# Graph layers with row gathers: one tile in 32 of the second layer is fetched row by row by SP and ACT instead of by POOL

## The reference, cut to what matters

```
h  = relu(layernorm(x))
m  = relu(concat(h[src], edge_attr) @ W_msg.T + b_msg)          # layer 0, per edge
m  = relu(m @ W_msg2.T + b_msg2)
x  = x + concat(h, segment_sum(m, dst) / count) @ W_apply.T + b_apply

h  = relu(layernorm(x))
a  = softmax of edge_weight over the edges of one dst           # layer 1, per edge
agg = segment_sum(a[:, None] * h[src], dst);  agg = agg / (|agg| + 1e-9)
c  = 0.5 * (h @ W_self + b_self + agg @ W_nb + b_nb);  c = c / (|c| + 1e-9)
x  = x + layernorm(c) * gamma + beta
```

## Time and profile before

| | |
|---|---|
| median of 3 runs | 11857.36 us |
| span of the profiled execution | 8618.0 us |
| the profiled execution's own time | not given beside its span |
| layer 1, gathers | 4389.7 to 8438.8 us |
| busy in the span: POOL, PE, DVE, ACT | 6262.0, 4989.1, 4066.7, 1112.8 us |

### The profile page before, as it was taken

The page is one execution under the profiler, slowest core; times in us unless marked ns, Lnnn a source line. Parts: engine busy times, 40 slices in busy tenths (PEclk is TensorE's granted clock), DMA queues, the critical chain, the costliest instruction groups (busy, mean ns, idle before and its releaser), DMA issues.

```text
span 8618.0 us, 124772 instructions
## 1 busy us (share of the span) xinstructions
PE 4989.1 (58%) x31459; PEld 4420.3 (51%) x31459; DVE 4066.7 (47%) x14617; ACT 1112.8 (13%) x1842; POOL 6262.0 (73%) x6528
## 2 busy tenths in 40 slices
PE   4777777777777777777744444444444444444444
PEld 3666666666666666666643333333333333333333
DVE  7555555555555555555553333333333333333336
ACT  2222222222222222222210000000000000000001
POOL 2777777777777777777657777777777777777772
PEclk9999999999999999999965555555555555555555
DMA  5332323233223333333332222222222222222222
GB/s 169 86 77 74 80 74 78 78 79 78 74 73 80 78 80 78 80 85 105 76 101 65 65 67 64 54 53 53 53 53 53 53 53 53 53 53 53 53 53 70
DMA packets 393788, 614.77 MB, mean 71 GB/s; under 512 B 171659, under 2 KB 249223, under 8 KB 392839
## 3 DMA queue, kind: packets, MB, share of 16 engines
q0 software_dynamic: 206848, 424.04, 19.2%
q1 hardware_dynamic: 186888, 190.15, 8.0%
HBM read 577.78 MB, written 35.92 MB: 71 GB/s over the span
## 4 chain that ended last, share of the span: by engine, by line
POOL 69%; issue 25%; PE 2%; DVE 2%; DMA 1%; DVEq 0%; SPq 0%; POOLq 0%; ACT 0%; ACTq 0%
POOL rows_ring L446 69%; PE bank L900 1%; PE bank L1028 0%; DVE acc L620 0%; DVE acc L609 0%; DMA rows_ring<-p_table,idx 0%; POOLq L191 0%; DVE stat L592 0%; SPq L338 0%; DVEq L609 0%; DVE acc L841 0%; DMA idx<-in_src_ring 0%; PE bank L891 0%; DVE work L874 0%; PE bank L897 0%
## 5 line engine op out<-in xcount | busy, mean ns | idle before, releaser
L446 POOL DMA_INDIRECT rows_ring<-p_table,idx x3232 | 3141.5, 972 | 1130.5 <-issue 1122.1
L446 POOL DMA_INDIRECT rows_ring<-h_table,idx x3232 | 3065.7, 949 | 1028.2 <-issue 984.3
L766 DVE TENSOR_TENSOR acc<-acc,bank 128x128 f32 x6464 | 1820.5, 282 | 2517.4 <-PE bank L900 2501.4
L900 PE MATMUL bank<-onehot,rows_ring 128*128 128x128 f32 x6464 | 1649.2, 435 | 2339.8 <-DMA rows_ring<-h_table,idx 2339.8
L900 PEld LDWEIGHTS bank<-onehot,rows_ring 128*128 128x128 f32 x6464 | 1417.4, 323 | 2571.6 <-issue 2242.3
L769 DVE TENSOR_SCALAR onehot<-iota,dloc,coef 128x128 f32<-128x128 f32 x6464 | 2286.3, 355 | 1.3 <-issue 1.2
L782 DVE TENSOR_TENSOR work<-bank,rows_ring 128x512 f32<-128x512 f32 x808 | 558.5, 691 | 1922.0 <-DMA rows_ring<-p_table,idx 1565.8
L900 PE MATMUL bank<-onehot,work 128*128 128x128 f32 x6464 | 935.1, 288 | 245.8 <-DVE onehot L769 239.2
L900 PEld LDWEIGHTS bank<-wmat,work 128*128 128x128 f32 x7264 | 983.4, 198 | 51.7 <-DVE acc L841 9.8
L900 PE MATMUL bank<-wmat,work 128*128 128x128 f32 x7264 | 987.7, 281 | 12.0 <-DVE acc L841 10.4
L900 PEld LDWEIGHTS bank<-onehot,work 128*128 128x128 f32 x6464 | 790.5, 193 | 387.4 <-DVE acc L766 348.3
(11 more groups left out here) (119 smaller groups left out, 782.9 us busy)
## 6 DMA issues: line engine op xcount, KB each, us to landing
work<-in_edge_t SPq DMA_DIRECT2D x404, 256.0 KB
rows_ring<-p_table,idx POOLq DMA_INDIRECT x3232
rows_ring<-h_table,idx POOLq DMA_INDIRECT x3232, 2.5
idx<-in_src_ring SPq DMA_DIRECT2D x404, 8.0 KB
ht_rows<-rows_ring SPq DMA_DIRECT2D x25, 256.0 KB, 2.1
p_table<-rows_ring SPq DMA_DIRECT2D x25, 256.0 KB, 2.2
work<-ht_rows SPq DMA_DIRECT2D x25, 256.0 KB, 2.6
h_table<-work SPq DMA_DIRECT2D x25, 256.0 KB, 2.3
```

What stands on the lines that cost most here:

```text
L446: pool.indirect_dma_start(out=rows_ring[:, 16 * h + G * k + j, :], out_offset=None, in_=table[:, :], in_offset=bass.IndirectOffsetOnAxis(a ...
L766: dve.tensor_tensor(win, win, ps_agg[k % 2][:, j * P:(j + 1) * P], ALU.add).then_inc(added, 1)
L900: ins = pe.matmul(tiles(dst)[t], left[t], right[t] if isinstance(right, list) else right, start=bias is None and n == 0, stop=n == len(pai ...
```

## The change

In layer 1 the last tile of every superblock (the fourth of its eighth group) isn't gathered by POOL. Its 128 source numbers lie in a new input `src_last`, one line of 128 per superblock. SP loads this line into one of two slots of `last_idx` (part of one partition). SP fetches the rows of the first 64 edges, in two lots of 32, ACT those of the other 64: each loads four numbers into registers, issues four transfers of one row each to `last_rows` (two slots of [128, 128]), and so on. PE takes the tile from there and waits for both engines' semaphores. The loops of PE, ACT and SP in layer 1 now hold two superblocks a turn; ACT's goes over all 101 superblocks (25 pairs of the self part, then 76 with the fetch alone).

```
+        def fetch_rows(eng, kind, by, h, at, n):
+            eng.sem_inc(S[by + "_turns"], 1)
+            for q in range(at, at + n, G):
+                _, nodes = nc.values_load_multi_w_load_instructions(
+                    last_idx[h][0:1, q:q + G], engines=[kind], min_val=0, max_val=N - 1, ...)
+                for j in range(G):
+                    eng.dma_start(last_rows[q + j:q + j + 1, h, :], h_table[ds(nodes[j], 1), :]).then_inc(s_last[by][h], 16)

 # SP
+            def load_last_idx(c, h):
+                sp.dma_start(last_idx[h], src_last[ds(c, 1), :]).then_inc(s_last_idx[h], 16)
+            load_last_idx(0, 0)
+            def body1(c, h, i, following=True):
+                if later(c):
+                    load_idx(1, 2 * c, 0, S["sums1_in_psum"])
+                sp.wait_ge(s_last_idx[h], 16 * i + 16)
+                if later(c, 2):
+                    sp.wait_ge(S["sums1_in_psum"], 8 * c - 8)
+                fetch_rows(sp, mybir.EngineType.SP, "sp", h, 0, P // 4)
+                if later(c):
+                    load_idx(1, 2 * c + 1, 1, S["sums1_in_psum"])
+                if following:
+                    if later(c):
+                        sp.wait_ge(S["sums1_in_psum"], 8 * c)
+                    load_last_idx(c + 1, 1 - h)
+                fetch_rows(sp, mybir.EngineType.SP, "sp", h, P // 4, P // 4)
...
-                if later(c):
-                    for half in range(2):
-                        load_idx(1, 2 * c + half, half, S["sums1_in_psum"])
+                body1(c, h, i)
...
-            with sp.Fori(NBATCH + 2, NPOOL) as i:
-                for h in range(2):
-                    load_idx(1, 2 * i + h, h, S["sums1_in_psum"])
+            with sp.Fori(0, (NPOOL - NBATCH - 2) // 2 - 1) as i:
+                body1(NBATCH + 2 + 2 * i, 1, NBATCH // 2 + 1 + i)
+                body1(NBATCH + 3 + 2 * i, 0, NBATCH // 2 + 2 + i)
...
 # POOL
-                        for j in range(G):
+                        for j in range(G - 1 if layer and h and k == 3 else G):
 # ACT
+            def body1(c, h, i):
+                act.wait_ge(s_last_idx[h], 16 * i + 16)
+                if later(c, 2):
+                    act.wait_ge(S["sums1_in_psum"], 8 * c - 8)
+                fetch_rows(act, mybir.EngineType.Activation, "act", h, P // 2, P // 2)
+
             def self_part(c, h, i):
+                body1(c, h, i)
                 act.wait_ge(S["h2_turned"], c + 1)
...
             pairs(act, self_part)
+            with act.Fori(0, (NPOOL - NBATCH) // 2) as i:
+                body1(NBATCH + 2 * i, 1, NBATCH // 2 + i)
+                body1(NBATCH + 1 + 2 * i, 0, NBATCH // 2 + 1 + i)
 # PE, layer1
-                        pe.wait_ge(s_rows[1][k], 64 * i + 64)
+                        if k < 7:
+                            pe.wait_ge(s_rows[1][k], 64 * i + 64)
+                        else:
+                            pe.wait_ge(s_rows[1][k], 48 * i + 48)
+                            pe.wait_ge(s_last["sp"][h], 16 * P // 2 * n + 16 * P // 2)
+                            pe.wait_ge(s_last["act"][h], 16 * P // 2 * n + 16 * P // 2)
+                            pieces[G - 1] = last_rows[:, h, :]
```

More of the change, by code:

```diff
@@ L51, with gnn @@
 BS = ["b_msg", "b2", "b_apply", "b_self", "b_nb", "gamma", "beta"]
-def gnn(nc, x, edge_t, src_ring, dst_halo, dst_tiles, tile_base, weight_flat, mats, we, rows, out):
+def gnn(nc, x, edge_t, src_ring, src_last, dst_halo, dst_tiles, tile_base, weight_flat, mats, we, rows, out):
     p_table = nc.dram_tensor("p_table", (NP, P), F32, kind="Internal").ap()
@@ L76, in gnn @@
         idx = sb("idx", [P, 2, 4 * G], I32)
+        last_rows = sb("last_rows", [P, 2, P])
         onehot = sb("onehot", [P, 2, G * P])
@@ L161, in gnn @@
         names = """weights_loaded counts_in_loaded soft_in_loaded tile_arrays_loaded pad_zeroed constants_made
-            vector_order pool_order pool_turns vector_turns
+            vector_order pool_order pool_turns vector_turns sp_turns act_turns
             bias_ready var0_ready root0_ready normed0_ready normed0_turned ht0_ready p_in_psum p_ready
@@ L179, in gnn @@
         s_idx = [S2["idx0_loaded"], S2["idx1_loaded"]]
+        s_last_idx = [sem(f"last_idx_loaded_{h}") for h in range(2)]
+        s_last = {e: [sem(f"last_rows_by_{e}_{h}") for h in range(2)] for e in ("sp", "act")}
+        last_idx = [rowk[0:1, h * P:(h + 1) * P].bitcast(I32) for h in range(2)]
         block = ctx.enter_context(nc.Block())
@@ L238, in live @@
             return not isinstance(i, int) or 0 <= 8 * i + k - lag < NG
+        def fetch_rows(eng, kind, by, h, at, n):
+            eng.sem_inc(S[by + "_turns"], 1)
+            for q in range(at, at + n, G):
+                _, nodes = nc.values_load_multi_w_load_instructions(
+                    last_idx[h][0:1, q:q + G], engines=[kind], min_val=0, max_val=N - 1,
+                    skip_runtime_bounds_check_because="sources are nodes")
+                for j in range(G):
+                    eng.dma_start(last_rows[q + j:q + j + 1, h, :], h_table[ds(nodes[j], 1), :]).then_inc(s_last[by][h], 16)
         class Order:
@@ L387, in beside1 @@
                     sp.dma_start(table_rows(self_rows, c - 2), four(self_out[h])).then_inc(S2["self_stored"][h], 16)
-                if later(c):
-                    for half in range(2):
-                        load_idx(1, 2 * c + half, half, S["sums1_in_psum"])
+                body1(c, h, i)
             pairs(sp, beside1, lag=2)
-            with sp.Fori(NBATCH + 2, NPOOL) as i:
-                for h in range(2):
-                    load_idx(1, 2 * i + h, h, S["sums1_in_psum"])
+            with sp.Fori(0, (NPOOL - NBATCH - 2) // 2 - 1) as i:
+                body1(NBATCH + 2 + 2 * i, 1, NBATCH // 2 + 1 + i)
+                body1(NBATCH + 3 + 2 * i, 0, NBATCH // 2 + 2 + i)
+            body1(NPOOL - 2, 1, (NPOOL - 2) // 2)
+            body1(NPOOL - 1, 0, (NPOOL - 1) // 2, following=False)
             for h in range(2):
@@ L552, in _ @@
             rounds(act, table_h2, 4)
+            for h in range(4):
+                act.wait_ge(S2["h2_stored"][h], 16 * used(4, h))
+            def body1(c, h, i):
[3 more added lines that the diff above has]
+                fetch_rows(act, mybir.EngineType.Activation, "act", h, P // 2, P // 2)
             def self_part(c, h, i):
+                body1(c, h, i)
                 act.wait_ge(S["h2_turned"], c + 1)
@@ L996, in _, with layer1 @@
             pe.wait_ge(S["coef_filled"], 2 * FILLS)
-            def layer1(i):
+            def layer1(i, h, n):
                 for k in range(8):
@@ L1001, in layer1 @@
                         g, slot = 8 * i + k, k % 2
-                        pe.wait_ge(s_rows[1][k], 64 * i + 64)
+                        pieces = [rows_ring[:, G * k + j, :] for j in range(G)]
+                        if k < 7:
[5 more added lines that the diff above has]
+                            pieces[G - 1] = last_rows[:, h, :]
                         pe.wait_ge(S["onehot1_ready"], g + 1)
@@ L1005, in layer1 @@
                             pe.wait_ge(S["sums1_added"], 4 * g - 4)
-                        products(ps_agg[slot][:, :], [([rows_ring[:, G * k + j, :] for j in range(G)], tiles(onehot[:, slot, :]))]).then_inc(S["sums1_in_psum"], 1)
+                        products(ps_agg[slot][:, :], [(pieces, tiles(onehot[:, slot, :]))]).then_inc(S["sums1_in_psum"], 1)
             def beside1(c, h, i):
@@ L1013, in beside1 @@
                 turn(ps_m1t[h][:, :], tiles(h2_in[h])).then_inc(S["h2_turned"], 1)
-                layer1(c)
+                layer1(c, h, i)
                 pe.wait_ge(S["h2t_ready"], c + 1)
@@ L1020, in _ @@
             pairs(pe, beside1)
-            with pe.Fori(NBATCH, NBODY) as i:
-                layer1(i)
+            with pe.Fori(0, (NBODY - NBATCH) // 2) as i:
+                layer1(NBATCH + 2 * i, 1, NBATCH // 2 + i)
+                layer1(NBATCH + 1 + 2 * i, 0, NBATCH // 2 + 1 + i)
             def norms(c, h, i):
@@ L1039, in _ @@
             rounds(pe, neighbours, 4)
-_ARGS = ["x", "edge_t", "src_ring", "dst_halo", "dst_tiles", "tile_base", "weight_flat", "mats", "we", "rows"]
+_ARGS = ["x", "edge_t", "src_ring", "src_last", "dst_halo", "dst_tiles", "tile_base", "weight_flat", "mats", "we", "rows"]
 def kernel(x, src, dst, edge_attr_64, edge_weight, L0_gnn_W_msg_w, L0_gnn_W_msg_b, L0_gnn_W_msg2_w, L0_gnn_W_msg2_b,
@@ L1062 @@
         "src_ring": c(src_pad.reshape(T // 16, 16, P).transpose(0, 2, 1)),
+        "src_last": c(src_pad.reshape(NPOOL, TILES_SB, P)[:, -1, :]),
         "dst_halo": np.stack([ends[p * LEN:p * LEN + LEN + 2] for p in range(P)]),
```

## The result

The change makes the kernel slower by about 15%: a median of 13,615.81 us (13,604.65 to 13,626.51) against 11,850.75 us, ratio 1.148 [1.146, 1.151]. I had forecast 11,958 us and a range up to 12,230. The sign was right, the size wrong by a factor of more than ten: +1765 us instead of +101.

What follows compares the result with a forecast made beforehand. POOL's gathers were taken to bound layer 1. Superblocks 26 to 101 at SP's period gave -27 us, the first 25 through ACT +128: +101 on 11,857, so 11,958 us, about 0.9% slower; range 11,680 to 12,230.

Steps and rivals of the forecast that it cites:

- The constant beside the span: Whole kernel: the 3239 us by which the median exceeds the profiled span stay constant, so span differences add to the median.
- longer gathers: Rival, whole kernel: the 3239 us belong to unprofiled gathers, pitch 1.754 us; the change gains 177 us, 11,680; chance 0.18.
- One issue: SP and ACT, layer 1: one single-row transfer with its register address work takes 0.48 us, bounds 0.33 and 0.58.
- F: Layer 1: fetching 64 rows costs SP and ACT each 36.9 us per superblock, bounds 27.3 and 43.3.
- SP at 39.75 us: SP, layer 1: its superblock takes 39.75 us, 0.9 above POOL's 38.85, setting superblocks 26 to 101: -27 us.
- The code term: SP and ACT loops, layer 1: jumping back over long bodies costs one code transfer, 2.5 us per turn, 1.25 per superblock.
- The ring through ACT: First 25 superblocks, layer 1: fetch, landing, PE's last group, self product and ACT's copy take 45.2 us each: +128 us.
- The removed gather: POOL, layer 1: one gather fewer in 32 saves 1.253 us a superblock, 127 us if nothing takes its place.
- Heavy: Rival, layer 1: SP and ACT streams bind everywhere, by three code transfers (12,210) or exclusive issues (12,610); chance 0.16.
- Both fit: Rival, layer 1: jump back costs little or nothing, issues cost their rows; +3 to +37 us, no measurable change; chance 0.22.
- faster: Rival, layer 1: SP and ACT streams are covered by POOL's gathers; 11,730, or 11,680 with gathers of 1.754 us; chance 0.28.
- the cover: Layer 1: fetching is hidden while SP stays below POOL's 38.85 us and ACT's cycle below 40.1, an issue below 0.42.

Runs made afterwards that it cites:

- comparisons 1, 3, 4 and 5: Rounds of timing in which kernels ran beside the kernel before, which took 8,624.10 us in the first, then 11,701, 11,705 and 11,893.97 us in the others named.
- the idle instructions: The kernel before plus 200 semaphore increments on ACT in each of layer 1's superblocks 26 to 101: 8,622.83 us (1.000); again, beside 11,705 us, 12,021.63 us (1.028).
- fixed rows: The change with its 128 single-row transfers at fixed addresses, without register loads or register work: 11,853.41 us, 1.014 of the kernel before.
- half the rows: The change with every second four rows left out on SP and ACT: 8,497.74 us (0.985 of before); again, beside 11,701 us, 11,827.89 us (1.010).

## Why the prediction was wrong

**The constant beside the span: the step that failed.** "I take them as a constant beside the span." Hardly 2 us lie beside it. The profiled execution of before, with its 8618 us, was one without slow stretches, and the executions of the median of 11,857 us were such with them, by all that the later ones show: one of 11,717.51 us has a span of 11,715.6. Every duration of the sum came from the first kind and was added to a time of the second. The rival "longer gathers" doubted the same premise, but stretched only the gathers and left SP's 39.75 us as they were; it came to 11,680 on the other side. The traces have it the other way round: the gathers keep their 945 ns, and the stream of small instructions on SP is what is stretched.

**One issue (0.48 us) and F (36.9 us): mis-sized by the same step.** Undisturbed they hold: 16 x 2.25 = 36 us, with 0.42 us from one row to the next. In the change's trace 32 rows take 30.7 to 33.5 us, so 64 take about 64 us instead of 36.9. The bounds, 27.3 and 43.3, were made from undisturbed rows only. The load of four was too low in any case (DVE's 343 ns against SP's 554 and ACT's 588), the single issue too high (228 and 213 against 288 ns); the two nearly cancel.

**SP at 39.75 us.** With some 64 for F, 3.5 for the index loads and what stands around them (1.6 + 1.32 + 2 x 0.29 in the timeline) and 1.25 of code it is 68.7 us; measured were 68.6. (The first load of each batch stands in the 3.5.) That SP's stream would reach POOL through its index loads was right. It does so everywhere, not only behind superblock 25, and by 29.8 us over the Pool's 38.85 instead of 0.9.

**The code term (2.5 us a turn): right.** Behind the branch SP and ACT stand still for 2.4 us (medians 2.36 and 2.35) where the body is some 430 instructions, with 524 packets on the instruction queue instead of 33; with bodies half as long it is 0.20 us and the queue is still. The Trainium skill (Runtime: NRT & Kernel Launch, Instruction fetch mechanics) states that a jump to a block that isn't held waits for a fetch; the traces agree, at 2.4 us a turn. But that is 1.2 us in 68.6.

**The ring through ACT (45.2 us, +128): not seen.** The first 25 superblocks take 1751 / 25 = 70.0 us each and the other 76 take 5183 / 76 = 68.2; SP's 68 us cover the ring, and without it the time is the same. Whether it would bind where there are no slow stretches wasn't measured. The 38.23 us that the forecast set beside it stand before ACT's copy L562, and not behind it.

**The removed gather (-127 us): right** at 8,624 us (-128.5), and -93 where before takes 11,701.

**The rivals.** "Heavy" had the outcome, SP binding everywhere, by causes that did not occur: the issues of both engines are no longer than one engine's, and the code costs as much as one transfer, not three. Its 12,610 was still 1000 us short. "Both fit" and "faster" are out. The runs bear out that the cover decides: with 32 rows for SP it nearly holds (1.010), with 64 it doesn't (1.152). The bound that the forecast gave for it, F below 33.0 us, leaves out its own code term (with it 31.8); nothing in the outcome rests on that.

**What stays open.** First, what the change does where before takes 8,624 us: in each of the five comparisons that held it before took 11,700 us or more. By the undisturbed parts SP would need about 36.1 + 1.6 + 1.2 = 38.9 us a superblock, an estimate, beside the Pool's 38.85. Second, what the slow stretches are. The traces show that they come in both layers, space out the instructions of PE, DVE, ACT and SP but not POOL's gathers, and go with the whole of a comparison rather than with a kernel. Nor do they go with the chip: the record gives the same one for comparisons 1, 3, 4 and 5, and only the first was without them. They end, in the trace of the idle instructions, with POOL's last gather, so they may hang on the gathers' transfers; no run changes these to see. The time doesn't follow the number of instructions alone either: fixed rows (138,754 instructions) and half the rows (146,837) both end 1.0 to 1.4% behind before, and in both SP hardly waits (10.3 us and none of 2700), though it has 64 and 104 instructions of a fetch a superblock instead of 208. The executions with stretches also hold fewer semaphore records (256 a superblock in layer 0 instead of 689, in the two traces of before). That makes the recording itself a suspect, and it isn't cleared: every execution listed comes with a span and a granted clock, and no run here shows one without records.

## What to carry to other kernels

Set the profiled execution's own time against the median before its durations are used. If they differ by far more than the runs differ among themselves (here 8,618 against 11,827 to 11,895), the profile may show another kind of execution than the one that is timed, and the difference need be no constant: the range has to hold the case that the added instructions are stretched by it. And when work is moved to an "idle" engine, count the instructions that it adds there: SP and ACT got 208 each in place of one gather of POOL's, and SP's stand around the two index loads for which POOL waits. An engine is idle only until its own later work is due: ACT's added instructions held up the kernel's end.

## What the runs showed of the hardware that was not expected

- Slow stretches in which SP's instructions take 0.7 us or twice that and PE's start 1.4 us or more apart, while POOL starts a gather every 1.25 us as ever: 16 rows took 9.41 us outside and 35.36 us within one. The same kernel takes 8,624 us without them and 11,700 to 11,900 with them.
- In such executions 200 added instructions a superblock on an idle engine cost 317 us, 211 of them because that engine came late to its own last part; a block of 200 took 46 to 90 us instead of 13.5, and 13.5 again behind the last gather. Without the stretches they cost nothing (1.000 [0.999, 1.001]).
- A single-row transfer at a register's address costs 228 ns of SP and 213 ns of ACT; a load of four registers costs 554 and 588 ns. From row to row pass 0.42 us on SP.
- A jump back over a body of 448 or 424 instructions leaves SP or ACT standing for 2.4 us; over one of 240 instructions, 0.2 us.
- TensorE was granted 0.98 of its clock in layer 0 without the stretches, 96% of the time at 2.4 GHz, and 0.72 with them, 45% at 2.4 and 55% at 1.2 GHz; in them its matmuls stand singly, with 1 to 2 us idle between.
